# Third key block's exponentials kept in float32, low parts of keys and queries on DVE, small maxima work on POOL, and another order of steps

## The chip, the cores and the metric

The kernel runs as one program on one core of a Trainium2 chip. The metric is the device time of a run in microseconds. The time of the kernel before is 1110.21 us, the median of three runs (1105.31, 1110.21, 1114.2). One further execution was taken with the profiler on.

## What is computed

Eight sequences of 512 tokens with 128 channels go through one transformer layer with its norms behind the sums. The attention has 16 heads of 64, is causal, and has one learned null key and null value that every query sees. Behind it comes a mixture of 32 experts (four chosen per token, with a capacity) and a shared expert. The change touches the attention:

```python
q = (x @ Wq).reshape(Bx, Tx, H, D).transpose(0, 2, 1, 3)
k = (x @ Wk).reshape(Bx, Tx, H, D).transpose(0, 2, 1, 3)
v = (x @ Wv).reshape(Bx, Tx, H, D).transpose(0, 2, 1, 3)
k = jnp.concatenate([k, jnp.broadcast_to(null_k, (Bx, H, 1, D))], axis=2)
v = jnp.concatenate([v, jnp.broadcast_to(null_v, (Bx, H, 1, D))], axis=2)
...
att = jnp.where(causal, att, jnp.finfo(att.dtype).min)
w = jax.nn.softmax(att, axis=-1)
y = jnp.einsum('bhts,bhsd->bhtd', w, v)
...
x = _layernorm(x + _L0_attn_ref(x, L0_attn_Wq, L0_attn_Wk, L0_attn_Wv, L0_attn_Wo, L0_attn_null_k, L0_attn_null_v, L0_attn_logit_scale), axis=-1)
```

## The kernel before

**Parts of numbers.** Products that need more than 16 bits are done in pieces. A float32 tensor is split into a float16 high part and a float16 low part (the difference, rounded), and a product is the sum of three float16 products: high by high, high by low, low by high. So it is with the projections (L896, L916), the scores (K1, K2, Q1, Q2 hold high and low parts stacked on the partitions) and the product of exponentials and values (L971 to L973).

**Heads and units.** Attention is done head by head, 128 heads in all (eight sequences of 16), and four heads make a unit (32 units). For each head the 512 queries are met with the causal part of the 512 keys, in blocks of 128: key block 0 meets 512 queries, block 1 384, block 2 256, block 3 128, together 1280 columns. In the tile PF the third key block (number 2, counted from 0) lies in columns 1024 to 1279, and it is the score segment 2 (`SEGS`).

**Stages of a head.** (1) The row maxima: four products of queries by keys (L927) in three PSUM fillings, which DVE adds to the causal mask and reduces (L1299). (2) For a unit the maxima are joined with the null score (L1307), negated (L1312), the null term is formed (L1317), the negated maxima are turned by PE (L935), copied by ACT (L1147) and moved by DMA into a row of Q2, so that the scores come out of PE with the maximum already taken off. (3) The scores with keys on the partitions (L950, L952 for the mask, L953), in three segments. (4) ACT takes the exponential of each segment into PF, float32 (L1160). (5) ACT copies all 1280 columns to PH, float16 (L1166), and DVE and POOL form PL = PF - PH: DVE columns 0 to 255 (L1324), POOL the other 1024 (L1623). (6) PE multiplies: for each of ten blocks of 128 x 128 three products with 65 or 64 moving columns (L971 to L973); the 65th column of VH is one and gives the sum. (7) DVE adds the null's share, takes the reciprocal and scales (L1332, L1338, L1347), and after the fourth head of a unit it multiplies the reciprocals by the null's exponentials (L1350).

**Keys and queries.** For a unit there are four projections of 512 tokens (K and Q, two pairs of heads each). ACT copies the high part out of PSUM (L1131), PE subtracts the high part in PSUM by a product with a negative identity, NID16 (L902), and ACT copies what is left as the low part (L1136). Then SP issues six DMAs that lay out K1 and K2, or Q1 and Q2 (L1730).

**What sets the order.** `plan` writes one list of steps, and every engine executes those that concern it in this order. A step of time is one head. `ORDER`, `ORDER2`, `ORDER3` and `ORDER4` say in which order the pieces of a step stand, for heads 0, 1, 2, 3 of a unit. At step n the maxima are those of head n + 7 (`LM`), the scores those of head n, high and low parts those of head n - 1, the values those of head n - 2, and the take-over by DVE ("take y") that of head n - 3. "place" and "slow" let one piece of the side work advance: the turning of the outputs, the output product, the null's maxima, and once per sequence the norm, the gate and the routing (`finish`). This side work shares one PSUM bank, MISC, which `take` and `release` hand on after a distance `HOLD`. POOL does its part of PL, the reciprocal root of the variance, and starts the scatters of token rows by indirect DMA (L1647). PF, PH and PL have three buffers (`PBUF`).

**After the attention** come the shared expert, the 32 experts and the final norm; no line of that part is touched.

Of the kernel before, what the change touches and what calls it, by code (L numbers as in the profile page):

```python
# [30 lines left out]
PBUF = 3  # L31
PSPLIT = 256
# [14 lines left out]
ORDER2 = (("take y",), ("scores", 0), ("max", 0), ("place",), ("take y",), ("project qk",), ("copy v",),  # L47
         ("high p",), ("place",), ("take y",), ("max", 1), ("project v",), ("place",), ("high qk",), ("slow",),
         ("scores", 1), ("scores", 2), ("low p",), ("max", 2), ("place",), ("slow",), ("place",),
         ("values", 0, 1, 2), ("low qk",), ("values", 3), ("place",), ("slow",), ("copy qk",), ("slow",),  # L50
         ("slow",))
ORDER3 = (("take y",), ("scores", 0), ("copy v",), ("max", 0), ("place",), ("place",), ("place",), ("take y",),
         ("high p",), ("take y",), ("project qk",), ("high qk",), ("max", 1), ("scores", 1), ("slow",),
         ("scores", 2), ("place",), ("project v",), ("slow",), ("max", 2), ("slow",), ("place",), ("low qk",),
         ("values", 3), ("copy qk",), ("place",), ("slow",), ("values", 0, 1, 2), ("slow",), ("low p",))
ORDER4 = (("copy v",), ("scores", 0), ("take y",), ("place",), ("take y",), ("max", 0), ("place",),
         ("project qk",), ("place",), ("high p",), ("take y",), ("high qk",), ("slow",), ("scores", 1),
         ("place",), ("max", 1), ("scores", 2), ("project v",), ("slow",), ("max", 2), ("low p",), ("slow",),
         ("slow",), ("place",), ("low qk",), ("copy qk",), ("values", 3), ("values", 0, 1, 2), ("place",),
         ("slow",))  # L60

# [1756 lines left out]
```

## Time and profile before

| | us |
|---|---|
| median of 3 runs | 1110.21 |
| the profiled execution's own time | 1116.88 |
| its span | 1114.7 |
| PE busy in the span | 896.7 |
| DVE busy | 739.9 |
| ACT busy | 664.6 |
| POOL busy | 610.3 |

The busy figures are sums over a span of two different halves. The page's second part, the span in 40 slices, shows them: up to about 750 us, the attention, PE and DVE are at 8 or 9 tenths in nearly all slices and ACT at 7 or 8; afterwards, in the experts, PE is at 5 to 7 tenths, POOL at 4 to 6, and DVE and ACT at 1 or 2. A busy PE is not PE at its peak, because the profile draws each product up to its last result while the next one is already running; the distance between the starts of two products tells what one costs.

### The profile page before, as it was taken

The page shows a single profiled execution, that of the slowest core. Times are in us where ns is not written, and L with a number is a line of the kernel's source. Part 1 is how long each engine was busy: PE and PEld are TensorE (multiplying, and loading weights), DVE is VectorE, ACT ScalarE, POOL GpSimd, SP SyncE. Part 2 cuts the span into 40 slices and gives each one's busy share as a digit, 9 for nine tenths or more (in the row PEclk, how much of TensorE's full clock was granted, in tenths as well). Part 3 has the DMA queues.
Part 4 walks back from the last instruction along what each step waited for, and adds up shares of the span by engine and source line. Part 5 has one row for each costly group of instructions (what it writes and reads, how often), then busy time and mean ns, then how long its engine had stood idle before and what let it go on. Part 6 is the DMA issues. An engine that isn't in the chain of part 4 may idle for free.

```text
span 1114.7 us, 25910 instructions
## 1 busy us (share of the span) xinstructions
PE 896.7 (80%) x9035; PEld 660.3 (59%) x9035; DVE 739.9 (66%) x2612; ACT 664.6 (60%) x1267; POOL 610.3 (55%) x518
## 2 busy tenths in 40 slices
PE   5769999899899999999999989865666766676626
PEld 2346677677677777767767767754444545454412
DVE  3557878998998998998998998982532222122106
ACT  4467887797787888788888878651212222222214
POOL 6033334366557557557547637755416656665655
PEclk9889999999999999999999999995878877787668
DMA  5565577554234434434433424004023434333237
GB/s 145 169 203 169 158 208 197 134 137 104 77 95 101 103 76 115 106 75 106 106 82 90 113 69 106 30 5 149 26 78 106 116 93 114 95 111 97 61 126 277
DMA packets 100466, 126.21 MB, mean 113 GB/s; under 512 B 18708, under 2 KB 61163, under 8 KB 99313
## 3 DMA queue, kind: packets, MB, share of 16 engines
q1 hardware_dynamic: 91120, 107.70, 35.1%
q0 software_dynamic: 9216, 16.86, 4.8%
q8 instruction: 72, 1.18, 0.5%
q14 instruction: 58, 0.47, 0.1%
HBM read 33.96 MB, written 42.24 MB: 68 GB/s over the span
## 4 chain that ended last, share of the span: by engine, by line
PE 42%; DVE 19%; another core or an unknown queue 12%; ACT 9%; issue 8%; DMA 5%; SPq 4%; POOL 1%; ACTq 0%; DVEq 0%; POOLq 0%
PE PS L1074 5%; PE PS L927 4%; DVE JUNK L1299 4%; PE PS L896 4%; SPq L1730 3%; PE PS L953 3%; PE PS L950 3%; DMA Q<-QL 2%; PE PS L916 2%; PE PS L971 2%; ACT PH L1166 2%; PE PS L972 2%; PE PS L973 2%; DVE NMD L1317 2%
## 5 line engine op out<-in xcount | busy, mean ns | idle before, releaser
L1623 POOL TENSOR_TENSOR PL<-PF,PH 128x1024 f16<-128x1024 f32 x128 | 275.9, 2155 | 321.9 <-ACT PH L1166 308.0
L1299 DVE CUSTOM_DVE_ANT_0 JUNK<-PS,M 128x512 f16<-128x512 f32 (+3 forms) x512 | 237.3, 485 | 56.6 <-PE PS L927 55.4
L1160 ACT ACTIVATE PF<-PS 128x512 f32<-128x512 f32 (+1 forms) x384 | 187.6, 527 | 66.0 <-PE PS L953 54.4
L1656 POOL DMA_INDIRECT y_rows<-BIG,Q x160 | 155.8, 973 | 107.8 <-ACT BIG L1213 65.8
L1166 ACT ACTIVATE PH<-PF 128x1280 f16<-128x1280 f32 x128 | 161.9, 1265 | 0.0
L927 PE MATMUL PS<-K,Q 128*128 128x512 f16 (+3 forms) x512 | 132.8, 305 | 31.8 <-DMA Q<-QL 20.3
L950 PE MATMUL PS<-Q,K 128*128 128x512 f16 (+3 forms) x512 | 151.7, 305 | 5.4 <-ACT PF L1160 5.2
L1647 POOL DMA_INDIRECT xe_rows<-PAY,DEST x128 | 128.2, 1002 | 44.4 <-issue 31.2
L953 PE MATMUL PS<-Q,K 128*128 128x512 f16 (+3 forms) x512 | 148.9, 304 | 0.0
L971 PE MATMUL PS<-VH,PH 128*128 128x65 f16 x1280 | 138.4, 196 | 9.5 <-DVE Y L1347 8.9
L973 PE MATMUL PS<-VH,PL 128*128 128x65 f16 x1280 | 138.6, 195 | 0.0
L972 PE MATMUL PS<-VL,PH 128*128 128x64 f16 x1280 | 138.6, 195 | 0.0
L971 PEld LDWEIGHTS PS<-VH,PH 128*128 128x128 f16 x1280 | 120.6, 98 | 15.1 <-issue 10.6
L972 PEld LDWEIGHTS PS<-VL,PH 128*128 128x128 f16 x1280 | 119.4, 99 | 12.9 <-issue 0.8
L1074 PE MATMUL PS<-PF,K 128*128 128x320 f32 x256 | 96.5, 531 | 35.0 <-DVE K L1553 26.1
L973 PEld LDWEIGHTS PS<-VH,PL 128*128 128x128 f16 x1280 | 119.8, 99 | 0.0
L1324 DVE TENSOR_TENSOR PL<-PF,PH 128x256 f16<-128x256 f32 x128 | 111.8, 873 | 2.6 <-ACT PH L1166 2.4
L952 PE MATMUL PS<-LATER,IDB 128*128 128x128 bf16 x512 | 113.2, 221 | 0.0
L1205 ACT ACTIVATE Y<-PS 128x640 f32<-128x640 f32 x32 | 22.6, 706 | 128.8 <-remote 67.8
L1553 DVE TENSOR_TENSOR K<-PS,Y 128x640 f32<-128x640 f32 x32 | 26.4, 825 | 107.5 <-PE PS L1074 40.9
L1074 PEld LDWEIGHTS PS<-PF,K 128*128 128x128 f32 x256 | 56.6, 232 | 63.2 <-issue 52.6
L927 PEld LDWEIGHTS PS<-K,Q 128*128 128x128 f16 x512 | 48.6, 99 | 62.3 <-issue 23.8
(220 smaller groups left out, 2074.8 us busy)
## 6 DMA issues: line engine op xcount, KB each, us to landing
K<-KH SPq DMA_DIRECT2D x128, 128.0 KB, 2.4
Q<-QH SPq DMA_DIRECT2D x128, 128.0 KB, 2.4
xe_rows<-PAY SPq DMA_DIRECT2D x20, 520.0 KB, 3.8
Q<-xe_rows SPq DMA_DIRECT2D x32, 325.0 KB
K<-KL SPq DMA_DIRECT2D x64, 128.0 KB, 2.4
Q<-QL SPq DMA_DIRECT2D x64, 128.0 KB, 2.4
y_rows<-PAY SPq DMA_DIRECT2D x16, 512.0 KB, 4.9
K<-in_L_ffn_w_dram SPq DMA_DIRECT2D x96, 64.0 KB
```

Source lines behind the costliest of these rows:

```text
L927: i = e.matmul(PS[:, 2 + k, c0:c0 + 128 * (q + 1)], Q1[:, u % 4, ab, pp, q * 128:(q + 1) * 128], K1[:, u % 4, ab, pp, 0:128 * (q + 1)], st ...
L950: e.matmul(PS[:, k, o:o + LEN[i]], K1[:, u % 4, ab, pp, block], Q1[:, u % 4, ab, pp, i * 128:512], start=True, stop=False)
L953: r = e.matmul(PS[:, k, o:o + LEN[i]], K2[:, u % 4, ab, pp, block], Q2[:, u % 4, ab, pp, i * 128:512], start=False, stop=True)
L971: e.matmul(PS[:, 4, o:o + 65], PH[:, n % PBUF, p], VH[:, vs, i, h, :], start=(i == 0), stop=False)
L972: e.matmul(PS[:, 4, o:o + 64], PH[:, n % PBUF, p], VL[:, vs, i, h, :], start=False, stop=False)
L973: r = e.matmul(PS[:, 4, o:o + 65], PL[:, n % PBUF, p], VH[:, vs, i, h, :], start=False, stop=(i == q))
L1074: i = e.matmul(PS[:, bank + hf, 0:320], EW[:, x_ % 4, m, :], XET[:, x_ % 2, hf * 320:(hf + 1) * 320], start=True, stop=True)
L1160: e.activation(PF[:, n % PBUF, c0:c0 + width], PS[:, k, 0:width], ACT.Exp).then_inc(s["c_exp"], 1)
L1166: e.activation(PH[:, n % PBUF, :], PF[:, n % PBUF, :], ACT.Copy).then_inc(s["c_hc"], 1)
L1299: e.tensor_tensor_reduce(JUNK[:, n_ttr % 2, 0:width], PS[:, 2 + k, c0:c0 + width], M0[:, 512 - width:512], 1.0, -3e38, ALU.add, ALU.max, M ...
L1623: e.tensor_tensor(PL[:, n % PBUF, PSPLIT:1280], PF[:, n % PBUF, PSPLIT:1280], PH[:, n % PBUF, PSPLIT:1280], ALU.subtract).then_inc(s["c_lp ...
L1656: e.indirect_dma_start(out=y4[:, :], out_offset=bass.IndirectOffsetOnAxis(ap=XE[:, x_ % 6, k, 128:129].bitcast(I32), axis=0), in_=OUT[:, x ...
```

## The change

- **The third key block** is no longer split. The exponentials in columns 1024 to 1279 stay in PF as float32, and the two blocks of 128 x 128 in it each meet the values in one float32 product, with V32, a float32 copy of the values of key block 2 (with its column of ones). DVE makes V32 from PSUM once per unit. PH and PL have 1024 columns. DVE's part of PL is gone; POOL still does 1024 columns. The high part waits for two segments of exponentials instead of three. The exponentials of head n now wait for the values of head n - 3, which read PF.
- **Low parts of keys and queries**: the product with the negative identity (L902) and ACT's copy (L1136) are gone. DVE subtracts the high part from PSUM.
- **Small work to POOL**: negated maxima, the null term and the null's shares ("shares") are issued by POOL. The null term now stands behind the turning of the maxima, with a pause of its own.
- **The norm after the attention** is applied by ACT instead of DVE, as x * rs + (-mean * rs); POOL forms the last term with two more small instructions.
- **The order**: all four tables are written anew, `HOLD` goes from 4 to 5, `NGP` from 4 to 6, x of the next sequence is loaded three steps earlier and its null scores are formed one step earlier. The old tables have 30 entries each and the new ones 29, as "low qk" is gone; one of the four is shown in part below.

```diff
-PSPLIT = 256
+
+WHOLE, SPLIT = 2, 1024
...
-HOLD = 4
-NGP = 4
+HOLD = 5
+KQ_AT = (-12, -11, -10, -9)
+V_AT = (-2, -1)
+X_AT = (-20, -15, -15)
+NULL_AT = 5
+NGP = 6
...
-ORDER = (("copy v",), ("take y",), ("take y",), ("scores", 0), ("max", 0), ("take y",), ("place",),
-         ("project v",), ("high p",), ("place",), ("max", 1), ("place",), ("project qk",), ("slow",),
-         ("high qk",), ("scores", 1), ("scores", 2), ("place",), ("low p",), ("max", 2), ("slow",), ("slow",),
-         ("place",), ("values", 0, 1, 2), ("low qk",), ("values", 3), ("copy qk",), ("slow",), ("slow",),
-         ("place",))
...
+ORDER = (("take y",), ("copy v",), ("scores", 0), ("take y",), ("high p",), ("max", 0), ("project v",), ("take y",),
+         ("slow",), ("place",), ("place",), ("slow",), ("project qk",), ("high qk",), ("max", 1), ("scores", 2),
+         ("scores", 1), ("slow",), ("max", 2), ("copy qk",), ("place",), ("place",), ("place",), ("slow",),
+         ("values", 0, 1, 2), ("place",), ("slow",), ("low p",), ("values", 3))
...
-    def proj_qk_low(u, kind, pp):
-        step("low qk", u, kind, pp, hold[u, kind, pp])
-        mark("lo", u, kind, pp, by="c_pj")
-
     def proj_qk_copy(u, kind, pp):
         k = hold[u, kind, pp]
         step("copy qk", u, kind, pp, k)
-        mark("cp", u, kind, pp, by="c_aj")
+        mark("cp", u, kind, pp, by="c_dj")
...
+        if half == WHOLE // 2:
+            mark("vw", u, half, by="c_dj")
+            pj_free[k] += (("vw", u, half),)
...
-        mark("ng", u, by="c_dr")
-        yield
-        step("max null", u)
-        mark("nm", u, by="c_dr")
+        mark("ng", u, by="c_ng")
+        yield
         yield from pause(NGP)
         yield from take()
         step("max turn", u, free)
@@ -251,6 +250,9 @@
         release(("mrow", u))
         mark("mdma", u, by="c_mrow", n=64)
         yield
+        step("max null", u)
+        mark("nm", u, by="c_nm")
+        yield from pause(NULL_AT)
...
+        step("shares", u)
+        mark("sh", u, by="c_sh")
...
-        dv("normalize")
+        dv("normalize", by="c_na")
...
-    PH = sb("PH", [128, PBUF, 1280], F16)
-    PL = sb("PL", [128, PBUF, 1280], F16)
+    PH = sb("PH", [128, PBUF, SPLIT], F16)
+    PL = sb("PL", [128, PBUF, SPLIT], F16)
+    V32 = sb("V32", [128, 2, 4, 65], F32)
...
-            elif name == "low qk":
-                u, kind, pp, k = a
-                hi = KH if kind == "k" else QH
-                w.wait_ge(*at("hi", u, kind, pp))
-                e.matmul(bank_of_proj(k), NID16[:, :], hi[:, pp, :], start=False, stop=True,
-                         skip_group_check=True).then_inc(s["c_pj"], 1)
...
                 w.wait_ge(*at("hc", n))
-                w.wait_ge(*at("lc", n))
                 w.wait_ge(*at("lp", n))
+                w.wait_ge(*at("exp", n, 2))
+                w.wait_ge(*at("vw", u, 1))
...
                         p = slice(OFF[i] + 128 * (q - i), OFF[i] + 128 * (q - i) + 128)
+                        if i == WHOLE:
+                            r = e.matmul(PS[:, 4, o:o + 65], PF[:, n % PBUF, p], V32[:, vs, h, :], start=False, stop=(i == q))
+                            continue
                         e.matmul(PS[:, 4, o:o + 65], PH[:, n % PBUF, p], VH[:, vs, i, h, :], start=(i == 0), stop=False)
                         e.matmul(PS[:, 4, o:o + 64], PH[:, n % PBUF, p], VL[:, vs, i, h, :], start=False, stop=False)
                         r = e.matmul(PS[:, 4, o:o + 65], PL[:, n % PBUF, p], VH[:, vs, i, h, :], start=False, stop=(i == q))
...
-            elif name == "copy qk":
-                u, kind, pp, k = a
-                lo = KL if kind == "k" else QL
-                w.wait_ge(*at("lo", u, kind, pp))
-                e.activation(lo[:, pp, :], bank_of_proj(k), ACT.Copy).then_inc(s["c_aj"], 1)
...
-                w.wait_ge(*at("lc", n - PBUF))
                 w.wait_ge(*at("lp", n - PBUF))
+                w.wait_ge(*at("pv", n - PBUF))
                 e.activation(PF[:, n % PBUF, c0:c0 + width], PS[:, k, 0:width], ACT.Exp).then_inc(s["c_exp"], 1)
...
-                e.activation(PH[:, n % PBUF, :], PF[:, n % PBUF, :], ACT.Copy).then_inc(s["c_hc"], 1)
+                e.activation(PH[:, n % PBUF, :], PF[:, n % PBUF, 0:SPLIT], ACT.Copy).then_inc(s["c_hc"], 1)
...
+            elif name == "normalize":
+                b, = a
+                w.wait_ge(*at("rs", b))
+                w.wait_ge(s_wl, 3)
+                w.wait_ge(s_wh, 3)
+                w.wait_ge(*at("uh", 0))
+                w.wait_ge(*at("ul", 0))
+                w.wait_ge(*at("wgt", 0))
+                for q in range(4):
+                    i = e.activation(X1[:, 4 * b + q, :], XA[:, b % 2, q, :], ACT.Identity, bias=SH1[:, q:q + 1],
+                                     scale=RS[:, q:q + 1])
+                i.then_inc(s["c_na"], 1)
...
+                if half == WHOLE // 2:
+                    o = 256 * (WHOLE % 2)
+                    e.tensor_copy(V32[:, u % 2, :, 0:64],
+                                  bank_of_proj(k)[:, o:o + 256].rearrange("p (h d) -> p h d", h=4)).then_inc(s["c_dj"], 1)
+            elif name == "copy qk":
+                u, kind, pp, k = a
+                hi, lo = (KH, KL) if kind == "k" else (QH, QL)
+                w.wait_ge(*at("hi", u, kind, pp))
+                w.wait_ge(*at(kind + "dma", u - 1))
+                e.tensor_tensor(lo[:, pp, :], bank_of_proj(k), hi[:, pp, :], ALU.subtract).then_inc(s["c_dj"], 1)
...
-                e.tensor_tensor(PL[:, n % PBUF, 0:PSPLIT], PF[:, n % PBUF, 0:PSPLIT], PH[:, n % PBUF, 0:PSPLIT],
-                                ALU.subtract).then_inc(s["c_lc"], 1)
...
+            elif name == "max negate":
+                u, = a
+                w.wait_ge(*at("mfin", u))
+                w.wait_ge(*at("mT", u - 2))
+                e.tensor_scalar(negated(u), MM[:, u % 2, :, :], -1.0, None, ALU.mult).then_inc(s["c_ng"], 1)
+            elif name == "max null":
+                u, = a
+                w.wait_ge(*at("ng", u))
+                w.wait_ge(*at("pn", u - 2))
+                e.tensor_tensor(four(NMD, u), negated(u).rearrange("p q (ab pp) -> p q ab pp", ab=2), null_of(u), ALU.add).then_inc(s["c_nm"], 1)
+            elif name == "shares":
+                u, = a
+                b, g = divmod(u, 4)
+                w.wait_ge(*at("y", 4 * u + 3))
+                w.wait_ge(*at("rT", b - 2))
+                e.tensor_tensor(ratios(b)[:, :, 4 * g:4 * g + 4].rearrange("p q (pp ab) -> p q pp ab", pp=2),
+                                RD[:, u % 2, :, :].rearrange("p (pp ab) q -> p q pp ab", pp=2),
+                                PN[:, u % 3, :, :].rearrange("p q (ab pp) -> p q pp ab", ab=2),
+                                ALU.mult).then_inc(s["c_sh"], 1)
...
-                e.tensor_tensor(PL[:, n % PBUF, PSPLIT:1280], PF[:, n % PBUF, PSPLIT:1280], PH[:, n % PBUF, PSPLIT:1280],
-                                ALU.subtract).then_inc(s["c_lp"], 1)
+                e.tensor_tensor(PL[:, n % PBUF, :], PF[:, n % PBUF, 0:SPLIT], PH[:, n % PBUF, :], ALU.subtract).then_inc(s["c_lp"], 1)
...
-                w.wait_ge(s_ve0, b + 1)
-                e.tensor_tensor(RS[:, :], VE[:, :], MHALF[:, :], ALU.pow).then_inc(s["c_pg"], 1)
+                w.wait_ge(s_ve0, 2 * b + 1)
+                e.tensor_tensor(RS[:, :], VE[:, :], MHALF[:, :], ALU.pow).then_inc(s_rs0, 1)
+                e.tensor_scalar(NME[:, :], MV[:, :, 0], -1.0, None, ALU.mult).then_inc(s_ve0, 1)
+                w.wait_ge(s_rs0, b + 1)
+                w.wait_ge(s_ve0, 2 * b + 2)
+                e.tensor_tensor(SH1[:, :], NME[:, :], RS[:, :], ALU.mult).then_inc(s["c_pg"], 1)
```

PE, at the end of a step, in the steady part. V is V32; the float32 product has the line L973 now, and K, Q, VH, VL, PH, PL are as above. Before, the last part of "values" for a head:

```order
L916 MATMUL PS<-WVH,XL 128x256
L927 MATMUL PS<-K,Q 128x256
L902 MATMUL PS<-QH,NID 128x512
L971 MATMUL PS<-VH,PH 128x65
L972 MATMUL PS<-VL,PH 128x64
L973 MATMUL PS<-VH,PL 128x65
L971 MATMUL PS<-VH,PH 128x65
L972 MATMUL PS<-VL,PH 128x64
L973 MATMUL PS<-VH,PL 128x65
```

And with the change, the end of "values" for a head, and what follows:

```order
L975 MATMUL PS<-VH,PH 128x65
L976 MATMUL PS<-VL,PH 128x64
L977 MATMUL PS<-VH,PL 128x65
L973 MATMUL PS<-V,PF 128x65
L935 MATMUL PS<-ID,NG 68x128 x4
L950 MATMUL PS<-Q,K 128x512
L952 MATMUL PS<-LATER,IDB 128x128
L953 MATMUL PS<-Q,K 128x512
```

The product with NID is gone from its place ahead of the values, and the block of PF comes as a single float32 product where three float16 ones stood.

DVE, around the take-over of a head's output, before (ISA is the masked row maximum and the reading of its result):

```order
L1324 TENSOR_TENSOR PL<-PF,PH 128x256
L1286 TENSOR_TENSOR VL<-PS,VH 128x512
L1332 TENSOR_TENSOR D<-PS,PN 128x4
L1338 RECIPROCAL RD<-D 128x4
L1299 ISA JUNK,MXV<-PS,M 128x512
L1299 ISA MXV 128x1
L1347 TENSOR_TENSOR Y<-PS,RD 128x4x64
```

And with the change:

```order
L1353 TENSOR_TENSOR Y<-PS,RD 128x4x64
L1311 TENSOR_TENSOR QL<-PS,QH 128x512
L1322 ISA JUNK,MXV<-PS,M 128x256
L1322 ISA MXV 128x1
L1337 TENSOR_TENSOR D<-PS,PN 128x4
L1299 TENSOR_TENSOR VL<-PS,VH 128x512
L1304 COPY V<-PS 128x4x64
```

The part of PL is gone from DVE; the low part of Q (or K) and the float32 copy of the values have come in.

POOL, over some two steps in which scatters are started, before:

```order
L1623 TENSOR_TENSOR PL<-PF,PH 128x1024
L1647 DMA xe_rows<-PAY,DEST 20480x130 x2
L1623 TENSOR_TENSOR PL<-PF,PH 128x1024
L1647 DMA xe_rows<-PAY,DEST 20480x130
L1623 TENSOR_TENSOR PL<-PF,PH 128x1024
```

And with the change:

```order
L1632 TENSOR_TENSOR PL<-PF,PH 128x1024
L1659 DMA xe_rows<-PAY,DEST 20480x130 x2
L1611 TENSOR_SCALAR NG<-MM 128x16
L1632 TENSOR_TENSOR PL<-PF,PH 128x1024
L1659 DMA xe_rows<-PAY,DEST 20480x130
L1616 TENSOR_TENSOR NMD<-NG,NS 128x16
L1632 TENSOR_TENSOR PL<-PF,PH 128x1024
L1659 DMA xe_rows<-PAY,DEST 20480x130
L1622 TENSOR_TENSOR R<-RD,PN 128x4x4
```

The small instructions on the maxima now stand between POOL's parts of PL.

## Rows read from the trace of the kernel before

**Rows 1.** The busy times by stretch: one sequence (us, engines' busy times, PEclk, DMA share, GB/s).
```profile
351.90:437.80 85.90, 80.98 (x1014) 61.59 (x1014) 79.43 (x299) 70.99 (x129) 52.25 (x39) 1.00 0.39 97
```

**Rows 2.** The chain of waits in that sequence, in order of time (start, us, what).
```profile
367.22 0.69 DVE JUNK L1299
369.24 2.07 DVE NMD L1317
375.93 0.39 PE PS L902
...
385.36 0.44 issue
392.92 0.41 PE PS L935 x4
395.35 0.65 PE PS L896 x3
...
410.81 0.69 DVE JUNK L1299
412.82 1.93 DVE NMD L1317
418.15 0.39 PE PS L902
...
433.50 0.69 DVE JUNK L1299
435.61 0.96 DVE PL L1324
436.57 1.24 issue
```

**Rows 3.** Groups of DVE from 150 to 740 us (busy us, mean ns of one).
```profile
L1324 DVE TENSOR_TENSOR PL<-PF,PH 128x256 f16<-128x256 f32 x109 | 90.0, 826 | 2.6 <-ACT PH L1166 2.4 <-issue 0.2
L1286 DVE TENSOR_TENSOR VL<-PS,VH 128x512 f16<-128x512 f32 x54 | 36.9, 683 | 3.0 <-ACT VH L1141 2.8 <-issue 0.2
L1317 DVE TENSOR_TENSOR NMD<-NG,NS 128x16 f32<-128x16 f16 x27 | 25.0, 927 | 0.0
L1388 DVE TENSOR_SCALAR X<-XA,MV,RS 128x128 f32<-128x128 f32 x28 | 17.9, 698 | 0.0
```

**Rows 4.** The instructions of line L1317 (duration min/median/max).
```profile
L1317 DVE TENSOR_TENSOR NMD<-NG,NS x32: 163/170/2285, 45.6 to 712.8; 128x16 f32<-128x16 f16 x32
```

**Rows 5.** Groups of ACT, the first two from 150 to 740 us.
```profile
L1166 ACT ACTIVATE PH<-PF 128x1280 f16<-128x1280 f32 x109 | 137.9, 1265 | 0.0
L1136 ACT ACTIVATE QL<-PS 128x512 f16<-128x512 f32 x50 | 29.8, 596 | 3.0 <-PE PS L902 3.0
...
L1220 ACT ACTIVATE PH<-PF,SB 128x128 f32<-128x128 f32 x32 | 13.0, 481 | 33.7 <-DVE SB L1577 30.6 <-DMA out_dram<-PH 3.1
```

**Rows 6.** PE's instructions in order of time, around the values of a head.
```profile
365.19 0.19 PE L971 MATMUL PS<-VH,PH 128*128 128x65 f16 x1
...
365.73 0.38 PE L902 MATMUL PS<-KH,NID 128*128 128x512 f16 x1
365.95 0.19 PE L971 MATMUL PS<-VH,PH 128*128 128x65 f16 x1
```

**Rows 7.** PE's instructions in order of time, around the gate's four float32 products.
```profile
539.85 1.03 PE L1019 MATMUL PS<-WGT,X1T 128*128 128x32 f32 x8
540.72 0.33 PE L950 MATMUL PS<-Q,K 128*128 128x384 f16 x1
```

**Rows 8.** Groups of PE's weight loads from 150 to 740 us.
```profile
L1000 PEld LDWEIGHTS PS<-WO,BIG 128*128 128x128 f32 x216 | 34.2, 191 | 3.2 <-ACT BIG L1171 0.2
```

**Rows 9.** Groups of POOL from 150 to 740 us.
```profile
L1623 POOL TENSOR_TENSOR PL<-PF,PH 128x1024 f16<-128x1024 f32 x109 | 235.2, 2158 | 220.3 <-ACT PH L1166 212.9 <-issue 6.8
L1647 POOL DMA_INDIRECT xe_rows<-PAY,DEST x96 | 96.8, 1009 | 19.8 <-issue 19.3 <-ACT PF L1160 0.3
```

**Rows 10.** The chain of waits near the start of the attention.
```profile
123.03 4.36 DMA Q<-QL
```

More of the change, by code:

```diff
@@ L52 @@
[L52 to L60, printed above, removed]
+HOLD = 5
@@ new lines @@
+ORDER2 = (("project v",), ("high p",), ("place",), ("project qk",), ("take y",), ("place",), ("max", 0), ("low p",),
+         ("take y",), ("scores", 0), ("place",), ("place",), ("take y",), ("slow",), ("max", 2), ("place",),
+         ("scores", 1), ("copy v",), ("slow",), ("slow",), ("max", 1), ("high qk",), ("scores", 2), ("slow",),
+         ("place",), ("copy qk",), ("slow",), ("values", 3), ("values", 0, 1, 2))
+ORDER3 = (("high p",), ("place",), ("copy v",), ("scores", 0), ("max", 1), ("take y",), ("take y",), ("project qk",),
+         ("take y",), ("high qk",), ("slow",), ("max", 0), ("place",), ("place",), ("copy qk",), ("slow",),
+         ("place",), ("place",), ("scores", 1), ("scores", 2), ("max", 2), ("project v",), ("values", 3), ("slow",),
+         ("slow",), ("slow",), ("low p",), ("place",), ("values", 0, 1, 2))
@@ L63 @@
+ORDER4 = (("take y",), ("place",), ("copy v",), ("place",), ("high p",), ("take y",), ("max", 0), ("place",),
+         ("project qk",), ("max", 1), ("high qk",), ("take y",), ("scores", 1), ("copy qk",), ("slow",), ("place",),
+         ("slow",), ("slow",), ("scores", 0), ("project v",), ("place",), ("place",), ("slow",), ("scores", 2),
+         ("values", 0, 1, 2), ("max", 2), ("low p",), ("slow",), ("values", 3))
 MAX_TILES = (((3, 0),), ((2, 0), (0, 384)), ((1, 0),))
@@ L554, in plan @@
                 run(qk)
-            elif name in ("high qk", "low qk", "copy qk"):
+            elif name in ("high qk", "copy qk"):
                 for fn, args in qk:
-                    {"high qk": proj_qk_high, "low qk": proj_qk_low, "copy qk": proj_qk_copy}[name](*args)
+                    {"high qk": proj_qk_high, "copy qk": proj_qk_copy}[name](*args)
             elif name == "place":
@@ L1162, in scalar @@
                 n, = a
-                for seg in range(3):
+                for seg in range(2):
                     w.wait_ge(*at("exp", n, seg))
                 w.wait_ge(*at("pv", n - PBUF))
-                e.activation(PH[:, n % PBUF, :], PF[:, n % PBUF, :], ACT.Copy).then_inc(s["c_hc"], 1)
+                e.activation(PH[:, n % PBUF, :], PF[:, n % PBUF, 0:SPLIT], ACT.Copy).then_inc(s["c_hc"], 1)
             elif name == "y copy":
@@ L1616, in gpsimd @@
                 w.wait_ge(s_k2, 4)
+            elif name == "max negate":
[17 more added lines that the diff above has]
+                                ALU.mult).then_inc(s["c_sh"], 1)
             elif name == "low p":
                 n, = a
-                for seg in range(3):
+                for seg in range(2):
                     w.wait_ge(*at("exp", n, seg))
```

75 lines of the change are left out of this document (21 added, 54 removed).

## The prediction, made before the run

> **What bounds the kernel now.** I read four views, in this order. The span in slices says where time is to be had: the attention up to about 750 us has two engines near their limit, and the experts behind it are untouched by the change, so some 365 of the 1115 us stay as they are. The busy times by stretch, taken over one sequence of 16 heads, give 85.9 us with DVE at 79.4, PE at 81.0, ACT at 71.0 and POOL at 52.3 [rows 1]. Two engines above nine tenths do not yet say which one is waited for. The chain of waits does: within the same sequence it leaves PE four times, from 367.22 to 375.93, from 385.36 to 392.92, from 410.81 to 418.15 and from 433.50 to 437.81, together 27.9 us, and runs over DVE, with ACT at the end of the first and the third [rows 2]. In the other 58 us PE works without a pause. So neither engine is the bound alone: PE for two thirds of the time, and DVE, which falls behind and then catches up, for one third.
>
> How much of the 85.9 us PE needs at the least follows from the distance between starts. A product of 512 columns takes 0.217 us (0.65 for three [rows 2]). Per head there are 7,168 float16 columns (1280 for maxima, 2560 for scores, 512 for masks, 1536 for one projection of K or Q, 512 for the negative identity, 768 for values), which is 14 such slots, 224 per sequence: 48.6 us. The 18 products between 365.19 and 365.73 take 0.03 us each [rows 6], so the 480 of a sequence take 14.4 us. Eight records of float32 products go by in 0.87 us, 0.11 each [rows 7]; a sequence has 124 of them (turns, output product, gate): 13.6 us. With 1 us of small turns PE needs 77.6 us, and 8.3 us of the 85.9 are waits.
>
> **The change part by part, per sequence.**
>
> *Third key block.* Two blocks of 128 x 128 per head, 6 float16 products at 0.03 us, become 2 float32 products. The trace has no float32 product with 65 columns. The gate's, with 32 columns, takes two records, 0.22 us [rows 7], and the output products with 128 columns keep the same pace, so the column count does not set it there. I take 0.22 us: 16 x (0.44 - 0.18) = **+4.2 us of PE**. From below it could be the price of the three float16 products it replaces, 0.09; from above, if the weights' load (0.19 [rows 8]) and the tail of the result (540.88 less 540.72, 0.16 us: 539.85 and 1.03 against the next start [rows 7]) are both exposed, 0.22 + 0.19 + 0.16 = 0.57 us. The gate's product is nearest in shape, hence the value. DVE loses its part of PL, 16 x 0.826 = 13.2 us, and gains V32, four copies of 256 columns from PSUM, between half and all of the 0.683 us of a subtraction of 512 [rows 3]; I take 0.4 each, 1.6 us. ACT's high part shrinks by 256 of 1280 columns, 0.25 us of 1.265 [rows 5], 4.0 us. POOL's part of PL stays at 1024 columns. The new wait of the exponentials for the values of head n - 3 costs nothing: PE has those values ahead of the scores of head n in its own order.
>
> *Low parts of K and Q.* PE loses 16 x 0.22 (365.73 to 365.95 [rows 6]) = **3.5 us**, ACT 16 x 0.596 = 9.5 us [rows 5]. DVE gains 16 subtractions of PSUM and SBUF with 512 columns, as for the values: 16 x 0.683 = 10.9 us [rows 3]. Three hand-overs (ACT, PE, ACT) become two (ACT, DVE), and the subtraction stands in the middle of the step instead of at its end, so SP can issue the last six moves of a unit some 2 us earlier. Five times between 80 and 190 us the chain holds a landing of Q's low part of 3 to 4.4 us [rows 10], while the fills run. I take 1 us each for them with some of the waiting moved elsewhere, -4 us in all; the ends are 0 and -19.
>
> *Small work to POOL.* The null term takes 0.170 us alone but up to 2.285 [rows 4], 0.927 in the mean [rows 3], and it stands twice in the chain, for 2.07 and 1.93 us [rows 2]. The long ones lie on top of POOL's part of PL, so they are waits. They leave DVE: 4 x 0.927 = 3.7 us. The negation and the shares leave it as well; I leave out their few tenths. POOL gets 14 more small instructions. Between the lone DVE time, 0.17, and POOL's own start of a scatter, 1.0 [rows 9], they cost 2.4 to 14 us, and POOL then stands at 66 of some 82 at most. Behind a waiting negation on POOL's queue stand the low part of the next head and two scatters. The low part has a whole step in hand before PE's values ask for it, so I cost this at nothing; without that slack a late low part would hold PE by its 2.16 us [rows 9] once per unit.
>
> *Norm.* DVE loses 4 x 0.698 = 2.8 us [rows 3], ACT gains 4 x 0.48 = 1.9 us [rows 5]. It is followed by the turn of x1 with six places between, so nobody waits.
>
> *The order* moves everything by fractions of a step. I find no queue on which a step has moved past the one it feeds; I price it at nothing and keep it as a rival.
>
> **The sum.** DVE: 79.4 - 13.2 - 3.7 - 2.8 + 10.9 + 1.6 = 72.2 us. ACT: 71.0 - 9.5 - 4.0 + 1.9 = 59.4. PE: 77.6 - 3.5 + 4.2 = **78.3**, which now is the longest by 6 us. The period lies between 78.3, where PE never waits (gain 7.6), and 86.6, where its 8.3 us of waits stay (loss 0.7). DVE falls behind by less in each step and has to catch up less; the time in which it holds the chain also loses the two null terms, 4.0 us, and gets back about a third of the added 12.5. I take half of PE's waits as gone: 78.3 + 4.1 = 82.4, a **gain of 3.5 to 4, say 4 us per sequence**. From 130 to 700 us there are 6.6 sequences: -26 us. The start gives -4. The last 12 heads have no projections to lose, only the float32 price, 12 x 0.26 = +3, against DVE work gone there too, 12 x 0.83, of which I count half, -5; -2 net. Together -32 us against the profiled execution's 1116.9 us (span 1114.7 and 2 around it): 1085. That execution stands 6.7 us above the median of the runs shown, so the forecast for the median is **1078 us**.
>
> **A rule against a row.** At the gate 32 float32 columns take as long as 128 elsewhere, 0.22 us [rows 7]. The Trainium skill, FP8 and Floating Point Precision, TensorE Precision Notes, counts a true float32 product as four passes through the array. By that count alone 65 columns would be four times the 0.03 us of a float16 product, 0.12 us, as an estimate. It would change the sum: that is the third rival.
>
> **Rivals.**
> 1. *PE alone is left.* For it: DVE has 6 us in hand and ACT 19. Against it: the maxima share two PSUM banks with DVE, so a hand-over can't vanish. 7.6 x 6.6 = 50, and up to 15 at the start, less 6.7: 1045 us. Chance 0.15.
> 2. *Nothing is gained.* The waits come from the alternation over two banks for the maxima and two for the scores, not from DVE's total; the new order puts them elsewhere. Against it: two null terms of 2 us stand in the chain. 0.7 x 6.6 - 4 = 0: 1110 us. Chance 0.17.
> 3. *A float32 product costs by its columns, four times a float16 one.* At 128 columns it does (0.22 us against a quarter of 0.217), and 65 columns would then cost 4 x 0.03 = 0.12 us instead of 0.22. For it: nothing here has 65 columns; against it: 32 columns were no faster [rows 7]. PE then needs 16 x 0.2 = 3.2 us less, 21 us in all, if the rest holds: 1057 us. Chance 0.08.
> 4. *Slower: the float32 product is exposed.* Each stands alone among products of 0.03 us, behind which its weights' load of 0.19 us [rows 8] can't hide, and the next ones must wait for it. At 0.57 us each, 256 of them cost 0.35 x 256 = 90 us more than I took: 1078 + 90 = 1168 us. It decides from 0.22 + (32 + 11) / 256 = 0.39 us on. Against it: the gate's four, with half the columns to hide behind, keep 0.22 us each [rows 7]. Chance 0.06.
>
> **Chances and range.** My forecast, from 1062 to 1098, has 0.54. About 1% (11 us) is what a measurement here can tell from no change. Faster by more than that, below 1099: 0.54 + 0.15 + 0.08, less a little for the upper edge, 0.76; within 1%: 0.17; slower: 0.07. The range from 1046 to 1108 takes in the third rival, reaches to the first, and covers most of what lies between the forecast and no gain; it leaves out the fourth rival and the upper part of the second.
>
> **What would show it.** In the changed profile a sequence in mid-attention is 82 us long, with DVE near 72 and ACT near 59. The float32 product (L973) has two records that lie 0.11 us apart. The low parts on DVE take 0.68 us, the null term on POOL is no longer in the chain, and the landing of Q's low part is gone from the chain before 190 us. The chain runs over PE for three quarters or more of a sequence. If a sequence is 86 us with DVE at 72, the order or the banks were the limit; if it is longer, L973 is the first place to look. A product of V32 with a distance above 0.39 us would make the prediction wrong, and so would a long wait of PE's values for POOL's low part.

## The result and the profile after

The changed kernel takes 1082.77 us (median of 4 runs, 1081.40 to 1083.34) against 1108.82 us before (4 runs): ratio 0.9752, interval 0.9725 to 0.9779. That is 26 us less; 1078 us were forecast, in a range from 1046 to 1108.

The busy times by stretch, for three sequences in mid-attention of the changed kernel, answer to [rows 1]:

```profile
309.00:392.70 83.70, 81.12 (x968) 65.13 (x966) 67.69 (x288) 62.33 (x116) 54.84 (x53) 1.00 0.41 100
392.70:477.20 84.50, 81.31 (x969) 64.94 (x966) 67.97 (x288) 62.45 (x116) 54.82 (x53) 1.00 0.40 99
477.20:561.40 84.20, 81.32 (x969) 65.02 (x966) 68.15 (x288) 62.40 (x117) 54.88 (x53) 1.00 0.40 99
```

A sequence takes 84 us instead of 86 to 88, PE's busy time is nearly unchanged (81.0 us before, 81.3 now), and DVE has dropped from 79.4 to 68 us. The measure used below is the period: the time between the same copy (PH) of heads 16 apart, as a mean over five sequences (heads 32 to 112). It is 87.2 us before and 84.0 after. The start gains more per sequence: from head 0 to head 32 it is 180.5 us before and 167.7 after, 12.8 us for two sequences. With 16 us from the next five, these two make up 29 of the 31 us by which the last PH copy comes earlier (746.1 to 715.2 us in the two traces). The experts' part behind it is nearly as long as it was (368.6 and 366.2 us). The two traced executions took 1116.88 and 1083.21 us, and the first stands 8 us above the median of its kernel. So differences between the traces are up to 8 us larger than the 26 us of the medians, and up to 1 us of the 3.2 us per sequence may be that execution's.

PE's instructions in order of time, around one float32 product (L973, two records) among the float16 ones:

```profile
401.19 0.30 PEld L973 LDWEIGHTS PS<-V,PF 128*128 128x128 f32 x2
401.22 0.41 PE L973 MATMUL PS<-V,PF 128*128 128x65 f32 x2
...
401.36 0.15 PEld L975 LDWEIGHTS PS<-VH,PH 128*128 128x128 f16 x1
401.47 0.19 PE L975 MATMUL PS<-VH,PH 128*128 128x65 f16 x1
```

From the start of the float32 product to the start of the next one are 0.25 us, 0.03 more than the gate's; so it is at each of the 97 places from 300 to 700 us where values follow (0.248 to 0.252). The three float16 products that it replaces took 0.09.

The groups of the moved work from 150 to 720 us (busy us, mean ns of one), answering to [rows 3, 5, 9]:

```profile
L1311 DVE TENSOR_TENSOR QL<-PS,QH 128x512 f16<-128x512 f32 x49 | 33.5, 685 | 0.0
L1304 DVE COPY V<-PS 128x256 f32<-128x256 f32 x27 | 11.2, 416 | 0.0
L1330 DVE TENSOR_TENSOR MM<-MXV,NS 128x16 f32<-128x16 f32 x26 | 6.3, 244 | 0.0
...
L1632 POOL TENSOR_TENSOR PL<-PF,PH 128x1024 f16<-128x1024 f32 x110 | 235.2, 2138 | 138.7 <-issue 79.3 <-ACT PH L1166 55.9 <-PE PS L973 1.7
L1611 POOL TENSOR_SCALAR NG<-MM 128x16 f16<-128x16 f32 x26 | 7.2, 279 | 21.6 <-DVE MM L1330 20.9 <-issue 0.2
L1622 POOL TENSOR_TENSOR R<-RD,PN 128x16 f32<-128x16 f32 x27 | 6.3, 235 | 1.8 <-DVE Y L1353 1.5
L1616 POOL TENSOR_TENSOR NMD<-NG,NS 128x16 f32<-128x16 f16 x26 | 5.9, 226 | 0.3
...
L1166 ACT ACTIVATE PH<-PF 128x1024 f16<-128x1024 f32 x110 | 115.5, 1050 | 1.3
L1186 ACT ACTIVATE X<-XA,SH,RS 128x128 f32<-128x128 f32 x28 | 11.5, 490 | 0.0
```

The small instructions cost 0.23 to 0.28 us each on POOL. On DVE the null term had taken 0.93 us in the mean.

The chain of waits in the sequence from 392.7 us, its longest pieces off PE, answering to [rows 2]:

```profile
417.06 0.70 DVE XA L1364
...
424.76 0.61 ACT X L1186 x2
426.98 0.95 ACT PH L1166
...
442.20 0.56 DVE JUNK L1322
444.39 0.60 DVE QL L1311
449.81 0.83 DVE GIF L1418
455.33 0.74 DVE I L1444 x5
458.94 0.60 DVE JUNK L1322
```

Neither the null term nor the parts of PL stand in it any more. What is left are two stretches, about 417 to 429 us (the sum for the norm on DVE, then the norm on ACT) and 442 to 459 us (the gate's routing on DVE, among low parts and maxima). The sequence that the prediction read had four. They are fewer, but longer. Over the five sequences of the period the chain of waits runs over PE for 51.6 us of 87.2 before and for 51.8 of 84.0 after, and over DVE for 24.5 and 20.9 us. The null term alone stood in it for 3.7 us per sequence before and for nothing after. So in the steady part the gain is about what the null term had held there, and the rest of the change comes out near zero.

### The profile page after: what moved, and what is told of

Read it like the earlier page. It is cut to its first block, busy times and chain, and to the rows that moved or that the text cites. A ratio compares the mean times of both kernels' runs of the same rounds, so it can differ in the third digit from the quotient of the medians.

```text
span 1081.4 us, 24722 instructions
## 1 busy us (share of the span) xinstructions
PE 885.5 (82%) x8651; PEld 677.9 (63%) x8651; DVE 647.0 (60%) x2517; ACT 592.5 (55%) x1171; POOL 630.6 (58%) x628
## 4 chain that ended last, share of the span: by engine, by line
PE 51%; DVE 14%; another core or an unknown queue 12%; issue 7%; ACT 6%; SPq 4%; DMA 3%; POOL 2%; ACTq 0%; DVEq 0%; POOLq 0%
PE PS L1078 5%; PE PS L927 5%; PE PS L973 4%; PE PS L902 4%; PE PS L950 4%; PE PS L953 4%; SPq L1742 4%; DVE JUNK L1322 3%; PE PS L916 2%; PE PS L975 2%; PE PS L977 2%; PE PS L976 2%; PE PS L1004 2%; PE PS L1005 2%
## 5 line engine op out<-in xcount | busy, mean ns | idle before, releaser
L1322 DVE CUSTOM_DVE_ANT_0 JUNK<-PS,M 128x384 f16<-128x384 f32 (+3 forms) x512 | 233.9, 483 | 71.5 <-PE PS L927 70.0
L927 PE MATMUL PS<-K,Q 128*128 128x384 f16 (+3 forms) x512 | 133.8, 304 | 31.3 <-DMA Q<-QL 20.6
L1166 ACT ACTIVATE PH<-PF 128x1024 f16<-128x1024 f32 x128 | 134.4, 1050 | 1.8
L975 PE MATMUL PS<-VH,PH 128*128 128x65 f16 x1024 | 126.5, 194 | 3.4 <-DVE Y L1353 3.4
L976 PE MATMUL PS<-VL,PH 128*128 128x64 f16 x1024 | 126.4, 193 | 0.0
L977 PE MATMUL PS<-VH,PL 128*128 128x65 f16 x1024 | 126.3, 193 | 0.0
L975 PEld LDWEIGHTS PS<-VH,PH 128*128 128x128 f16 x1024 | 106.1, 106 | 4.4 <-ACT PH L1166 2.6
L973 PE MATMUL PS<-V,PF 128*128 128x65 f32 x512 | 106.1, 289 | 0.0
L976 PEld LDWEIGHTS PS<-VL,PH 128*128 128x128 f16 x1024 | 95.7, 98 | 1.5
L977 PEld LDWEIGHTS PS<-VH,PL 128*128 128x128 f16 x1024 | 95.8, 98 | 0.0
L1217 ACT ACTIVATE Y<-PS 128x640 f32<-128x640 f32 x32 | 22.6, 706 | 133.4 <-remote 73.2
L927 PEld LDWEIGHTS PS<-K,Q 128*128 128x128 f16 x512 | 50.4, 103 | 65.8 <-issue 25.6
```

Source lines behind the costliest of these rows:

```text
L927: i = e.matmul(PS[:, 2 + k, c0:c0 + 128 * (q + 1)], Q1[:, u % 4, ab, pp, q * 128:(q + 1) * 128], K1[:, u % 4, ab, pp, 0:128 * (q + 1)], st ...
L973: r = e.matmul(PS[:, 4, o:o + 65], PF[:, n % PBUF, p], V32[:, vs, h, :], start=False, stop=(i == q))
L975: e.matmul(PS[:, 4, o:o + 65], PH[:, n % PBUF, p], VH[:, vs, i, h, :], start=(i == 0), stop=False)
L976: e.matmul(PS[:, 4, o:o + 64], PH[:, n % PBUF, p], VL[:, vs, i, h, :], start=False, stop=False)
L977: r = e.matmul(PS[:, 4, o:o + 65], PL[:, n % PBUF, p], VH[:, vs, i, h, :], start=False, stop=(i == q))
L1322: e.tensor_tensor_reduce(JUNK[:, n_ttr % 2, 0:width], PS[:, 2 + k, c0:c0 + width], M0[:, 512 - width:512], 1.0, -3e38, ALU.add, ALU.max, M ...
```

## The experiments

Twelve kernels ran in three sets of four, each set on a chip of its own. The time of the kernel before differs between the chips (1122.5, 1063.8 and 1118.9 us), so results are given as ratios to it. A point is 0.01 of such a ratio. The changed kernel was not measured again on these chips, so the distance in points between it and a run carries what the kernel before did on another chip. In the first and third sets that is 8 to 12 us: `e1_old_order` lies 20 us above the changed kernel by the ratios and 32 in plain time, `e2_split_pool` 21 and 12 us below it. The sizes in points are that uncertain; a sign changes only for `e7_split_negact`, 2 us below the changed kernel by the ratios and 7 above it in plain time. On the second chip the difference lies in the experts' part, 322.5 us instead of 368.6, by the traces of `b3_small_pool` and of the kernel before. What is left of the time before is then the same in both sets (741 and 740 us), so the second set's periods can be compared with 87.2. In the other two sets the experts' part is as long as in the first runs (366 to 371 us), but the kernel before took 10 to 14 us more, over 1 us per sequence; it was not traced there, and their periods are compared with 87.2 with that uncertainty. Absolute figures in the expectations are for the first runs' 1109 us.

| kernel | ratio to before (95%) | period, us |
|---|---|---|
| before | 1 | 87.2 |
| changed kernel | 0.9752 (0.9725 to 0.9779) | 84.0 |
| *taken back in the changed kernel:* | | |
| e1_old_order | 0.9929 (0.9899 to 0.9959) | 90.2 |
| e2_split_pool | 0.9563 (0.9508 to 0.9618) | 81.6 |
| e4_lowqk_back | 1.0198 (1.0144 to 1.0253) | 91.9 |
| e5_small_dve | 1.0081 (1.0047 to 1.0116) | 91.4 |
| *added to the kernel before:* | | |
| b1_new_order | 1.0409 (1.0377 to 1.0441) | 93.1 |
| b2_float32 | 1.0064 (1.0044 to 1.0084) | 88.8 |
| b3_small_pool | 0.9840 (0.9803 to 0.9878) | 83.3 |
| b4_lowqk_dve | 1.0378 (1.0339 to 1.0418) | 92.8 |
| *probes:* | | |
| e6_neg_act | 0.9955 (0.9930 to 0.9979) | 89.0 |
| e7_split_negact | 0.9736 (0.9710 to 0.9762) | 84.6 |
| e8_twice | 1.0010 (0.9989 to 1.0030) | 88.4 |
| e9_split_oldorder | 1.0055 (1.0027 to 1.0084) | 91.7 |

### The order taken back

```diff
-HOLD = 5
-X_AT = (-20, -15, -15)
-NGP = 6
+HOLD = 4
+X_AT = (-17, -15, -14)
+NGP = 4
...
-ORDER = (("take y",), ("copy v",), ("scores", 0), ...
+ORDER = (("copy v",), ("take y",), ("take y",), ("scores", 0), ...
```

> The changed kernel with the four order tables, HOLD, NGP and the loads of x as they were before. Theory A (the work moved off DVE and ACT shortens PE's waits; the order is worth little): 1085 to 1092 us, so most of the 26 us gain stays. Rival B (the new order is what gained): 1100 us or more.

Measured: 0.9929. Of the gain of 2.5%, 1.8 points go with the order, so theory A, that the order is worth little, fell here. In steady state the old order with the new work takes 90.2 us, 6 more than the changed kernel. The waits from 150 to 740 us of this kernel name the places (engine, line waited for: total us, times, longest):

```profile
POOL NG L1613 <- DVE MM L1332: 49.9, 22, 4.5
DVE VL L1301 <- ACT VH L1142: 29.7, 22, 3.7
PE PS L929 <- DMA Q<-QL: 22.6, 14, 2.7
```

POOL waits 49.9 us with its negation for DVE's maxima (20.9 us in the changed kernel), and PE's maxima wait 22.6 us for the landing of Q's low part (5.3 us in the kernel before, 2.5 in the changed one).

### The float32 block taken back

```diff
-WHOLE, SPLIT = 2, 1024
+WHOLE, SPLIT = 9, 1280
...
-    V32 = sb("V32", [128, 2, 4, 65], F32)
+    V32 = None
...
-                for seg in range(2):
+                for seg in range(3):
```

> The changed kernel, but the third key block is split into float16 parts again, and POOL forms the low part of all 1280 columns (none on DVE). PE loses 2 x 0.25 us and gains 6 x 0.03 us per head, 5.1 us per sequence, 41 us in all; ACT gains 4 us per sequence, POOL 9 us. Theory A (PE is the bound that is left, so the float32 block costs more than it gives): 1045 to 1068 us. Rival C (the float32 block pays because POOL's longer instruction holds DVE and comes later): 1083 us or more.

Measured: 0.9563, the fastest of all, 1.9 points or 21 us below the changed kernel by the ratios. In plain time it is 12 us below (1071.1 against 1082.8), and the two traces differ by 12 us as well. Theory A's direction holds; its 1045 to 1068 are met by the ratio (0.9563 x 1109 = 1061) and missed by 3 us in plain time. Two sequences of this kernel:

```profile
305.90:387.60 81.70, 77.27 (x1001) 60.03 (x1000) 67.97 (x286) 65.00 (x118) 62.96 (x53) 1.00 0.41 102
387.60:469.00 81.40, 76.39 (x997) 59.50 (x995) 67.14 (x282) 64.43 (x116) 62.08 (x52) 1.00 0.41 103
```

PE is at 77 instead of 81 us, POOL at 62.5 instead of 55, and DVE is no busier: POOL can take all 1280 columns. So the float32 block is a loss in this kernel against POOL's taking the columns, of half of PE's 5.1 us per sequence (period 84.0 to 81.6). PE is not what is left in it: the chain runs over PE for 31 us of the 81.6, over DVE for 25 and over ACT for 14.

### Low parts of keys and queries taken back

```diff
+            elif name == "low qk":
+                u, kind, pp, k = a
+                hi = KH if kind == "k" else QH
+                w.wait_ge(*at("hi", u, kind, pp))
+                e.matmul(bank_of_proj(k), NID16[:, :], hi[:, pp, :], start=False, stop=True,
+                         skip_group_check=True).then_inc(s["c_pj"], 1)
```

The step stands directly ahead of "copy qk", which is ACT's again.

> The changed kernel, but the low parts of keys and queries are made by PE's product with the negative identity and ACT's copy again. PE +3.5, ACT +9.5, DVE -10.9 us per sequence. Theory A (PE is the bound): PE's 28 us in all come back nearly whole, 1103 to 1112 us. Rival D (DVE's load sets the waits): 1080 us or less.

Measured: 1.0198, slower than the kernel before, 4.5 points above the changed one, and beyond theory A's 1103 to 1112 us (1.0198 x 1109 = 1131). PE's 3.5 us per sequence are less than half of the 7.9 us that the period grows. The waits from 150 to 740 us show the rest:

```profile
PEld PS L913 <- ACT QH L1146: 25.4, 28, 1.4
PEld PS L913 <- ACT KH L1146: 22.3, 36, 0.9
```

L913 is the product with the negative identity: it comes soon behind ACT's high part, and PE, which works in order, stands still until that is there. Its place was my choice, so the 4.5 points are an upper end for what DVE's subtraction gives. The mechanism, a hand-over to ACT and back inside PE's order, is seen. The start is lost too: from head 0 to head 32 this kernel takes 181.7 us, as much as the kernel before.

### Small work taken back to DVE

The three branches "max negate", "max null" and "shares" are moved from POOL's function to DVE's, their steps stay in place.

> The changed kernel, but negation, null term and shares are issued by DVE again, at the same places of the order. Theory A: DVE gets 12 small instructions per sequence, some of which wait up to 2.1 us for POOL's part of PL; 1 to 1.5 us per sequence, 1090 to 1096 us. Rival: they are hidden behind PE, 1083 us.

Measured: 1.0081. I had expected 7 to 13 us and it costs 3.3 points, 36 us. DVE's groups from 300 to 700 us:

```profile
L1335 DVE TENSOR_SCALAR NG<-MM 128x16 f16<-128x16 f32 x18 | 15.3, 851 | 0.0
L1340 DVE TENSOR_TENSOR NMD<-NG,NS 128x16 f32<-128x16 f16 x18 | 12.0, 669 | 0.0
L1346 DVE TENSOR_TENSOR R<-RD,PN 128x16 f32<-128x16 f32 x17 | 8.7, 512 | 0.0
```

The sum of one of each is 2.03 us per unit, 8.1 per sequence. Over the five sequences of the period DVE's instructions sum to 11.1 us more per sequence than in the changed kernel, as two of the routing's (OH and PO) grow by 3.0 us as well, and the period grows by 7.4. In the kernel before the negation and the shares took their lone 0.18 and 0.17 us; the new order puts them on top of POOL's part of PL. PE feels it: its waits for DVE's maxima (L927) are 37.3 us from 150 to 720 us against 8.1 in the changed kernel.

### The negation on ACT

Null term and shares are on DVE, as in the run above, and the negation is ACT's:

```diff
+            elif name == "max negate":
+                u, = a
+                w.wait_ge(*at("mfin", u))
+                w.wait_ge(*at("mT", u - 2))
+                e.activation(negated(u), MM[:, u % 2, :, :], ACT.Copy, scale=-1.0).then_inc(s["c_ng"], 1)
```

> The changed kernel with null term and shares on DVE, and the negation on ACT (Copy with scale -1). Against the run with all three on DVE (1.008 of before) only the negation has moved, off the engine that waits for POOL. Theory F (each wait of DVE for POOL's long instruction passes one for one into the period): 4 x 0.78 us per sequence on DVE go, some 20 us in all, 0.985 to 0.993 of before. Rival (the stalls are hidden, the loss comes from the queueing of dependent steps): 1.00 or more.

Measured: 0.9955, 1.3 points below `e5_small_dve`, 2.4 us of period for 3.4 us of negation taken off DVE (4 x 0.851). Theory F's sign is right; its 0.985 to 0.993 were too much. The shares now meet POOL more often (0.512 us each in `e5_small_dve`, 1.013 in this run).

### One part at a time, on the kernel before

The order alone, with the product with the negative identity ahead of its copy:

> The kernel before with nothing but the new order tables (the product with the negative identity put directly ahead of its copy), HOLD 5, NGP 6 and the earlier x. Theory A2 (order and moved work belong together; the new order puts small DVE work on top of POOL's long instruction, which the move to POOL made harmless): 1.00 to 1.04 of the kernel before. Rival B (the order gains by itself, as the 1.8% of the run with the old order suggests): 0.98 to 0.985.

Measured: 1.0409. The order that is worth 1.8 points in the changed kernel gains nothing in the old one with the product at this place, so rival B did not come true here. Two possible causes are seen, one among DVE's groups from 300 to 700 us, the other among PE's waits:

```profile
L1347 DVE TENSOR_TENSOR R<-RD,PN 128x16 f32<-128x16 f32 x17 | 15.8, 929 | 0.0
```

```profile
PEld PS L899 <- ACT QH L1128: 29.6, 27, 2.5
PE PS L899 <- ACT QH L1128: 20.1, 23, 2.0
```

The shares take 0.93 us instead of 0.17. PE's product L899 waits for ACT's high parts, 31 us in these 400 (20.1 for Q's, 11.2 for K's), or 7 us per sequence, at a place that again is my choice, and the period has grown by 5.9. So that place may account for all of the loss. How the loss divides between the two isn't settled, and the 4.1 points are an upper end for what the order costs in the old kernel.

The float32 block alone (`WHOLE`, V32, two segments for the high part, DVE's part of PL gone):

> The kernel before with the float32 third key block alone. Per sequence PE +5.1, DVE -11.6, ACT -4 us. Theory A2 (PE two thirds and DVE one third of the chain): +3.4 - 3.9, so 0.99 to 1.005 of before. Rival C (relief of DVE counts in full): 0.97 to 0.98.

Measured: 1.0064, slightly slower, where A2 gave 0.99 to 1.005: the relief of DVE by 11.7 us per sequence does not pay for PE's 5.1, though DVE is busier in this kernel than in the changed one. In the trace DVE's instructions sum to only 5.9 us less: those that are left wait longer, the null term 1.40 us in the mean instead of 1.01.

The small work on POOL alone (the three branches and their counters, the steps as before, "shares" ahead of the turning of y):

> The kernel before with negation, null term and shares on POOL alone, in the old order. Theory A2: the two null terms of 2 us per sequence leave the chain, up to 4 us per sequence, 0.975 to 0.985 of before. Rival E (negation queued behind POOL's low part and scatters comes late for the turn of the maxima, which PE waits for in order): 1.00 or more.

Measured: 0.9840, as A2 had it, and a period of 83.3 us, below the changed kernel's 84.0. In steady state this part alone gives all of the gain, which fits the null term's 3.7 us in the chain before. What it lacks is the start: head 0 to head 32 takes 181.1 us, as before (180.5), while the changed kernel needs 167.7. The run with the old order needs 171.5, so most of the start's 12.8 us comes with the other parts and not with the order; it is gone without the low parts on DVE (181.7 us in `e4_lowqk_back`), and these alone don't bring it (182.8 in `b4_lowqk_dve`).

The low parts on DVE alone:

> The kernel before with the low parts of keys and queries on DVE alone, in the old order. Per sequence PE -3.5, ACT -9.5, DVE +10.9 us, DVE then at some 90 of 86 us. Theory A2: DVE alone becomes the bound, 1.02 to 1.05 of before. Rival D2 (only PE and the hand-overs count): 0.97 to 0.98.

Measured: 1.0378. The busy times from 300 to 486 us, two sequences:

```profile
300.00:486.00 186.00, 159.17 (x2003) 119.99 (x2002) 177.96 (x635) 128.76 (x225) 103.97 (x76) 1.00 0.37 90
```

DVE is busy for 178 of 186 us, and of a sequence's 92.8 us the chain runs over DVE for 41.5 and over PE for 28. This part loses by itself, and by `e4_lowqk_back` it gains once DVE has been emptied.

### How far PE is the bound

```diff
-                            r = e.matmul(PS[:, 4, o:o + 65], PF[:, n % PBUF, p], V32[:, vs, h, :], start=False, stop=(i == q))
+                            for _ in range(2):
+                                r = e.matmul(PS[:, 4, o:o + 65], PF[:, n % PBUF, p], V32[:, vs, h, :], start=False, stop=(i == q and _ == 1))
```

> The changed kernel with each float32 product of the third block done twice into the same accumulation, so its output counts that block's share twice. 256 more products of about 0.25 us are 64 us of PE. Theory A (PE is the bound): 1.025 to 1.035 of before, nearly all of it shows. Rival C (PE has waits to spare): 1.00 or less.

Measured: 1.0010, 2.6 points above the changed kernel, 29 us for the 256 added products, between theory A and rival C. From the start of such a pair to the next product are 0.474 us, so the second one costs 0.224, the gate's price. They are 7.2 us of PE per sequence, and the period grows by 4.4. Doubling the products makes PE nearly full:

```profile
309.00:486.00 177.00, 175.99 (x2067) 144.49 (x2063) 137.06 (x575) 125.50 (x233) 109.54 (x104) 1.00 0.38 95
```

The chain now runs over PE for 79.4 us of the 88.4. So about 60% of this addition to PE shows, and 40% falls into its waits. With `e2_split_pool`, where PE's 5.1 us brought 2.4, about half of a microsecond taken from or added to PE reaches the period of the changed kernel.

### Two attempts on the best version

The float16 parts with the negation on ACT:

> The run with the third block in float16 parts and POOL's part of PL over 1280 columns (0.956 of before), with the negation on ACT instead of POOL. POOL's next low part no longer stands behind a wait for DVE's maxima. Theory A: PE is the bound, little changes, 0.950 to 0.958 of before. Rival (POOL's queue is late for the values): 0.945 or less.

Measured: 0.9736, slower by 1.7 points than with the negation on POOL. ACT's waits from 150 to 720 us:

```profile
ACT NG L1145 <- DVE MM L1333: 25.1, 8, 3.8
```

Both the theory and the rival had looked at POOL, and both were missed. What is queued behind the waiting instruction differs: on ACT an exponential comes next behind 31 of the 32 negations, on POOL a part of PL. That this is what decides is argued, not shown.

The float16 parts with the old order:

> The run with the third block in float16 parts (0.956 of before), with the old order tables, HOLD, NGP and x. It tells whether the new order is tied to the float32 block. Theory A2 (the order fits the low parts on DVE and the small work on POOL, both still there): 0.97 to 0.98. Rival (it was made for the float32 block): 0.955 or less.

Measured: 1.0055; I had expected 0.97 to 0.98. The order is worth 4.9 points with the float16 block, more than with the float32 one, so the rival is out, and theory A2 had it too small. In the old order the block's return costs 1.3 points (0.9929 to 1.0055), in the new one it gains 1.9. By the waits from 300 to 700 us of this kernel its negation on POOL waits for the maxima, with a part of PL behind it that now takes all 1280 columns:

```profile
POOL NG L1611 <- DVE MM L1330: 30.0, 9, 4.7
```

That this wait is the reason is argued, not shown.

## Why the prediction was right, and where it was not

**The place of the gain and its size** were right: 26 us measured, 31 forecast. That the null terms stand in the chain and that moving them pays was right and is shown by `b3_small_pool`. The bound was read rightly as shared, but from a sequence with more of PE than most: 58 us of 85.9, where the mean of five is 51.6 of 87.2. The rival "PE alone is left" did not come true (PE waits on), and neither did "nothing is gained". The sign "the chain runs over PE for three quarters or more" failed: it is 51.8 of 84.0 us, 62%.

**The period.** Forecast 82.4 us, measured 84.0. Of the 1.6 us, 1.0 is the mis-sized float32 product, 32 x 0.03, which puts the least that PE needs at 79.3 us; the other 0.6 are waits, 4.7 us instead of the 4.1 that were left. That half of PE's waits would go was an assumption, and that it came out so near is in part luck. The exposed weight load was a rival with 0.57 us per product; whatever is exposed costs 0.03 us, and only on the first of a pair (`e8_twice`). The third rival, by which 65 columns would cost 0.12 us, is out by the measured 0.25. The count of four passes in the Trainium skill (FP8 and Floating Point Precision, TensorE Precision Notes) does not give the price of a product this narrow; the measurement decides.

**DVE** was forecast at 72.2 us and stands at 68. V32 at 0.416 us and the low part at 0.685 were right. What the sum left out is, first, the negation and the shares, 1.4 us per sequence and not "few tenths", and then the waits for POOL that other small DVE instructions lost: the maxima with the null (L1330 now) fall from 0.433 to 0.242 us, the routing's scaling (from L1506) from 1.696 to 0.175 and its comparisons (EQ) from 0.565 to 0.187, all read from 300 to 700 us. One gained: the cast GIF rises from 0.164 to 0.705 us, and it stands in the chain.

**ACT** was forecast at 59.4 and stands at 62.4. The low-part copies and the high part's 0.215 us (1265 to 1050 ns) came out as read, save that the last was taken as 0.25, 0.6 us per sequence. Summed over its instructions ACT loses 10.8 us per sequence, against 11.6 forecast; its busy time falls by 8.7 only, because the drawn instructions overlap each other less than before.

**The start** was forecast at -4 us. It gives 12.8 us for two sequences, 6 more than the steady gain would. The landing of Q's low part does not leave the chain before 190 us, as was expected, but shrinks in it: before it was there five times with together 19.0 us, now three times with together 7.6.

```profile
81.03 2.37 DMA Q<-QL
...
159.35 2.81 DMA Q<-QL
...
182.94 2.39 DMA Q<-QL
```

Its worth had been taken near the lower end of the range (0 to -19).

**The step that failed** is "The order moves everything by fractions of a step. I price it at nothing". The order is worth 1.8 points in the changed kernel and 4.9 with the block in float16 parts. The sum came out near the truth although this term was missing and the float32 block by itself loses, so its total owes something to luck. Taken one at a time the parts are not terms of a sum: added singly, the float32 block, the small work, the low parts and the order give +0.6, -1.6, +3.8 and at most +4.1%, all together -2.5%. That each addition loads or frees DVE in places that only the matching order uses is how I read this; no run isolates it. The fifth part, the norm on ACT, was in no run taken back or added alone, and its price is open.

**POOL's small work** was booked as 3.7 us of DVE that leave. In the new order their place on DVE costs 7.4 us of period. In the old one it costs 3.9 (87.2 to 83.3), up to 1 us of it perhaps the traced execution's; the chain's two null terms of together 4.0 us had told this [rows 2].

## What to carry to other kernels

Small instructions on DVE that work from SBUF to SBUF may belong elsewhere when POOL runs long ones: look at the minimum and the maximum of one line, and at whether the long ones stand in the chain. Before trading several narrow float16 products for one float32 product, price it by its distance in a trace, 0.25 us here against 0.09 for three, and ask whether an idle engine can take the splitting instead. Parts of a change that move work between engines and the order that fits them must be tried together: two of the four parts lost by themselves, the order gained nothing in the old kernel, and the best kernel, 0.9563 of before, is the changed one without its first part.

## What the runs showed of the hardware

- A DVE instruction on 128 x 16 elements, 0.17 us alone, took 0.51 to 1.01 us in the mean where it met POOL's instruction of 2.14 us. A negation with a single SBUF tensor was held too (0.851 us), which I had not expected. In `e5_small_dve` 11 of the 32 negations took over 0.35 us; 10 of these started while POOL's part of PL ran and ended 0.04 us behind its end, and none of the other 21 started in one.
- A float32 product of 128 x 128 weights by 65 columns costs 0.25 us between float16 products of 0.03, with its two loads drawn at 0.30 us; a second one right behind it costs 0.224 (`e8_twice`).
- One chip of three ran the experts' part in 322.5 us instead of the 366 to 371 that the traces from elsewhere show; what the time before has left beside it is the same (741 and 740 us).
